# First stage of a fused conditional attention and MLP kernel: x blocks two and three requested behind the conditioning weights, the first transposes put into five banks, the second group's weights centred later

## The reference, cut to what matters

```
mod = swish(c) @ w_mod + b_mod            # six vectors of 576 for each of 2 batches
xn  = ln(x) * (1 + sc_msa) + sh_msa       # x: 2 x 2048 x 576
qkv = xn @ w_qkv + b_qkv                  # 16 heads of 36
q, k = ln(q, g_q), ln(k, g_k)             # over the 36 of a head
o   = softmax(q k^T / 6) v @ w_proj + b_proj
x   = x + g_msa * o
h   = gelu((ln(x) * (1 + sc_mlp) + sh_mlp) @ w1 + b1)
x   = x + g_mlp * (h @ w2 + b2)
```

## Time and profile before

| What | Value |
|---|---|
| Median of 3 runs (lowest, highest) | 2591.44 us (2589.94, 2591.81) |
| The profiled execution's own time | 2591.07 us |
| Its span on the core | 2589.3 us |
| PE busy | 2542.3 us, 98% of the span |
| DVE, ACT, POOL busy | 1871.6 us (72%), 1590.1 us (61%), 475.4 us (18%) |
| First score products of the attention on PE | at 97.33 us |
| First exponential on ACT | at 98.90 us |

### The profile page before, as it was taken

One profiled execution on the slowest core, in us unless ns is written; L12 is line 12 of the kernel. 1 busy time (PEld: TensorE's weight loads), 2 busy tenths in 40 slices (PEclk: granted clock), 3 DMA queues, 4 the chain that ended last, 5 costly groups with the idle time before them and its releaser, 6 DMA issues.

```text
span 2589.3 us, 41475 instructions
## 1 busy us (share of the span) xinstructions
PE 2542.3 (98%) x15223; PEld 1257.8 (49%) x15223; DVE 1871.6 (72%) x2950; ACT 1590.1 (61%) x2350; POOL 475.4 (18%) x334
## 2 busy tenths in 40 slices
PE   5999999999999999999999999999999999999999
PEld 3444444444444444444444433347566574756656
DVE  7788887788888788788777754275767667576743
ACT  4887787777777787888777776751423325142331
POOL 2532332223222222222322200001011010101100
PEclk9999999999999999999999999999999999999999
DMA  7513311223332133333111166356484856648443
GB/s 240 99 36 76 85 33 33 50 64 79 73 62 61 39 71 76 70 84 70 35 33 33 41 198 181 109 178 206 141 252 148 264 173 217 204 142 250 147 172 122
DMA packets 325888, 300.92 MB, mean 116 GB/s; under 512 B 235390, under 2 KB 267588, under 8 KB 313842
## 3 DMA queue, kind: packets, MB, share of 16 engines
q1 hardware_dynamic: 325394, 298.21, 41.4%
q10 hardware_dynamic: 288, 0.04, 0.0%
HBM read 203.84 MB, written 45.05 MB: 96 GB/s over the span
## 4 chain that ended last, share of the span: by engine, by line
PE 92%; DMA 2%; DVE 2%; SPq 1%; ACT 1%; issue 1%; POOL 0%; DVEq 0%; ACTq 0%
PE at_ps L1219 18%; PE at_ps L1202 17%; PE at_ps L2128 14%; PE at_ps L2085 14%; PE at_ps L1256 11%; PE at_ps L1230 8%; PE at_ps L1239 4%; PE at_ps L2056 4%; DMA ml_w_in<-in_L_cond_w 1%; PE at_ps L2078 1%; PE at_ps L2041 1%; DMA ml_held<-head_rden 0%; DMA st_wm_first<-in_L_cond_b_mod 0%; ACT at_aff L806 0%; PE at_ps L228 0%
## 5 line engine op out<-in xcount | busy, mean ns | idle before, releaser
L775 ACT ACTIVATE at_p<-at_ps 128x1024 f32<-128x1024 f32 x1024 | 1039.3, 1029 | 334.6 <-PE at_ps L1202 331.1
L1219 PE MATMUL at_ps<-at_p,at_v 128*37 128x512 f32 x2304 | 591.1, 593 | 0.0
L955 DVE TENSOR_TENSOR at_rest_of_p<-at_p,at_pr 128x1024 bf16<-128x1024 f32 x448 | 552.6, 1233 | 15.4
L642 POOL TENSOR_TENSOR at_tssq<-at_tssq,power 128x8 f32<-128x8 f32 x112 | 279.4, 2494 | 877.6 <-DVE at_tssq L918 877.0
L2085 PE MATMUL at_ps<-ml_xhi,ml_ring 128*128 128x512 f16 x1296 | 384.4, 381 | 2.9 <-ACT ml_g L1784 2.9
L2128 PE MATMUL at_ps<-ml_ring,ml_hid 128*128 128x288 f16 x3024 | 371.7, 286 | 0.8 <-issue 0.8
L947 DVE CAST at_pr<-at_p 128x1024 fp32r<-128x1024 f32 x448 | 315.2, 703 | 78.7 <-ACT at_p L775 77.6
L1230 PE MATMUL at_ps<-at_pr,at_vr 128*101 128x512 f32 x896 | 365.0, 488 | 1.3 <-DVE at_pr L947 1.2
L2128 PEld LDWEIGHTS at_ps<-ml_ring,ml_hid 128*128 128x128 f16 x3024 | 295.8, 98 | 75.9 <-issue 1.3
L1202 PE MATMUL at_ps<-at_qk_odd 109*64 109x512 f16 (+1 forms) x1658 | 309.4, 382 | 5.4 <-ACT at_p L775 5.4
L1202 PE MATMUL at_ps<-at_qk_even 109*64 109x512 f16 (+1 forms) x1536 | 308.7, 382 | 2.4 <-ACT at_p L775 2.4
(11 more groups left out here) (202 smaller groups left out, 2646.0 us busy)
## 6 DMA issues: line engine op xcount, KB each, us to landing
ml_ring<-w_halves SPq DMA_DIRECT2D x56, 1296.0 KB, 5.7
ml_ring<-w_halves SPq DMA_DIRECT2D x32, 1152.0 KB, 8.5
head_sums<-at_oT SPq DMA_DIRECT2D x256, 72.0 KB
ml_held<-head_sums SPq DMA_DIRECT2D x64, 256.0 KB
at_xy<-in_x SPq DMA_DIRECT2D x32, 288.0 KB, 2.9
ml_x<-in_x SPq DMA_DIRECT2D x8, 1152.0 KB, 10.2
w_halves<-ml_w_parts SPq DMA_DIRECT2D x18, 504.0 KB, 4.8
out<-ml_x SPq DMA_DIRECT2D x7, 1152.0 KB, 8.9
```

Of the source, the lines that this page charges most:

```text
L642: pool.tensor_tensor(tssq[:, 1, :], tssq[:, 1, :], keep.power[:, 0:QK], ALU.pow).then_inc(t_rstd, 1)
L775: act.activation(p[:, s % NP, :], ps[:, 2 * (s % 2):2 * (s % 2) + 2, :].rearrange("p a n -> p (a n)"), ACT.Exp).then_inc(exp_done, 1)
L955: nc.vector.tensor_tensor(rest_of_p[:, n % NL, :], p[:, s % NP, :], pr[:, n % NZ, :].bitcast(F32), ALU.subtract).then_inc(low_p_ready, 1)
L1219: last = nc.tensor.matmul(acc[a * HP:a * HP + RW, bank_of(U)], v32[:, (G % 2) * NT + 2 * s + a, h, :], p[:, s % NP, a * CH:(a + 1) * CH], ...
```

## The change

It edits five lists and one helper. SP: block 1 is requested when the first half of the conditioning weights has landed, block 2 behind it and ahead of group 1's weights, and block 3 ahead of `load_low`. PE: the transposes of block 0 write the banks 4, 5, 1, 2, 3 and wait for nothing; `product(0, 1)` stands ahead of block 1's first transposes; the last tile of block 0 is cut into two halves of 7 matmuls around the transpose of k = 4. DVE: block 1's statistics stand behind group 0's low parts, its normalising behind block 0's `low_x`, block 2's statistics earlier; `centre(1)` moves from behind block 0 to behind block 2, and `cut_low(1)` with its tail from the middle of block 2's `low_x` to behind `normal(0)`. ACT: `cut_high(1)` moves behind `square(1)`, and block 3's first cast waits for group 1's low parts, since it overwrites their place. POOL: block 1's `rstd_of` stands between the third and the fourth cast of block 0.

```
+        def turn_bank(t, k):
+            return 4 + (t * KC + k) % 2 if t else (4, 5, 1, 2, 3)[k]
@@ SP
             start.load_c(sp)
             load_x(0)
-            load_x(1)
             start.load_group(sp, 0)
             start.load_first(sp)
             sp.wait_ge(start.wm_loaded[0][0], 16)
+            load_x(1)
+            load_x(2)
             start.load_group(sp, 1)
-            load_x(2)
+            load_x(3)
             start.load_low(sp)
-            load_x(3)
             start.load_tail(sp)
@@ POOL
             rstd_of(0)
-            rstd_of(1)
             for k in range(KC):
                 pool.wait_ge(aff_ready, k + 1)
                 pool.tensor_copy(xhi[:, k, 0:CH], aff[:, k % 2, :]).then_inc(xhi_ready, 1)
+                if k == 2:
+                    rstd_of(1)
@@ ACT, affine
-                act.activation(aff[:, n % 2, :], ps[:, 4 + n % 2, :], ACT.Identity,
+                act.activation(aff[:, n % 2, :], ps[:, bank, :], ACT.Identity,
...
+                if t == NCH - 1 and k == 0:
+                    act.wait_ge(start.low, 2)
@@ ACT, the list
-            affine(1, 0)
-            affine(1, 1)
             raw(0)
-            affine(1, 2)
-            affine(1, 3)
-            affine(1, 4)
+            for k in range(KC):
+                affine(1, k)
             raw(1)
             square(0)
-            start.cut_high(act, 1)
-            start.cut_high_tail(act, 1)
...
             raw(3)
             square(1)
+            start.cut_high(act, 1)
+            start.cut_high_tail(act, 1)
             start.take_rows(act, 1)
@@ DVE
             stats_of(0)
-            stats_of(1)
             start.centre(dve, 0)
             normalise(0)
-            normalise(1)
             start.cut_low(dve, 0)
             start.cut_low_tail(dve, 0)
+            stats_of(1)
             for k in range(KC):
                 low_x(0, k)
-            start.centre(dve, 1)
-            start.gains(dve)
+            normalise(1)
+            stats_of(2)
             low_x(1, 0)
             low_x(1, 1)
-            stats_of(2)
             low_x(1, 2)
+            normalise(2, (0, 1))
             low_x(1, 3)
             low_x(1, 4)
-            normalise(2)
+            normalise(2, (2, 3))
+            start.gains(dve)
             sum_of(0)
@@ PE
-                    if n >= 2:
+                    if t:
                         pe.wait_ge(aff_ready, n - 1)
...
             first_product()
+            product(0, 1)
             turn(1, (0, 1))
-            product(0, 1)
+            product(0, 2)
             turn(1, (2, 3))
-            product(0, 2)
+            product(0, 3, range(0, 7))
             turn(1, (4,))
-            product(0, 3)
+            product(0, 3, range(7, 14))
```

More of the change, by code:

```diff
@@ L1139, in _ @@
             low_x(2, 4)
+            start.centre(dve, 1)
             normalise(3)
             normal(0)
+            start.cut_low(dve, 1)
+            start.cut_low_tail(dve, 1)
             sum_of(1)
```

15 lines of the change are left out of this document (7 added, 8 removed).

## The result

| | before | after |
|---|---|---|
| Median (12 executions each) | 2591.80 us | 2598.18 us |
| Lowest, highest | 2589.22, 2593.93 | 2595.67, 2599.98 |
| Profiled execution, its span | 2591.07, 2589.3 us | 2595.74, 2593.8 us |
| First scores on PE | 97.33 us | 99.94 us |
| First exponential on ACT | 98.90 us | 103.44 us |

A forecast was written before the change was run, and what follows sets the result against it. It took PE to hold 92% of the chain, with the stage going from wait to wait; +4.4 at conditioning, -0.8 POOL, -2.2 block 3's DVE list gave 1.4 us gained, so 2590.0 us, 8-in-10 range 2587.0 to 2592.9.

The forecast's parts named there:

- Conditioning: Start of the stage: PE finishes the conditioning products at 25.15 instead of 29.52, 4.4 us earlier.
- the bound of 26.3: Block 1's x on DVE: landing after 26.3 us decides for the case of a slower kernel.
- The slower rival: Block 1's x lands late, delaying DVE's statistics and the first `xlo`; 2592.0, or 2593 with 10 us; 17%.
- POOL's root: Block 1's add and power between POOL's third and fourth casts make block 0's fifth piece 0.8 us late.
- 0.45 to the end of the first tile: PE in block 0: after the last `low_x`, 0.45 us to finish the first token tile.
- PE falls to the slow pace: Rival: PE's clock drops in the thin stretch between 25 and 35 us, 0.7 us off the gain, 2590.7; 5%.
- Five banks: PE's transposes of block 0 into five banks: costed at nothing, `xlo` pieces still every 1.20 us.
- Block 3's list: DVE's work behind `centre(1)`, 12.35 us, ends at 75.1, so `affine(3, 2)` comes 1.4 us earlier than before.
- POOL's powers come at their old distance from DVE's sums: End of the stage: POOL's powers keep their old delay behind DVE's sums, with no cost added.
- Behind `affine(3, 2)` the change leaves every list as it was: From `affine(3, 2)` to the scores nothing changes, so only that start is asked for; 1.4 us gained.
- Nothing arrives: Rival: waits in DVE's late list or POOL's power of `sum_of(1)` cost 1.4 more; 2591.4; 20%.
- The main account: Late centring in block 3's DVE list takes back the rest of the front's lead, leaving 1.4 us.

The follow-up runs named there:

- e3: Changed kernel with 14 extra matmuls filling the waits of PE's first product in block 0; median 2598.26 us, ratio 1.0024 to the kernel before.
- e11: Changed kernel with block 1's root behind the casts, `sum_of(1)` ahead of `cut_low(1)`, `vr` cleared later, and the filling matmuls of e3 and e6; ratio 1.0007.
- e12: e11 with `centre(1)` on DVE ahead of block 2's low parts instead of behind them; ratio 1.0002 to the kernel before.
- e10: Kernel before the change, with POOL clearing `vr` five times instead of once, between power(1) and power(2); ratio 1.0013.
- e2: Changed kernel with DVE doing `sum_of(1)` ahead of `cut_low(1)` and its tail instead of behind them; ratio 1.0014 to the kernel before.
- e4: Kernel before with only the late centring: `centre(1)`, `cut_high(1)`, `cut_low(1)` moved, block 3's first cast waiting; median 2599.39 us, ratio 1.0026.
- e6: Changed kernel with 16 extra matmuls on PE between the first and third score products; ratio 1.0016 to the kernel before.

## Why the prediction was wrong

It forecast 2590.0 with 2587.0 to 2592.9, no change to be told. Each row of the table is a stretch in which a term of it went wrong. The lead over the kernel before, in us:

| Place | Predicted | Measured | Lost on the way |
|---|---|---|---|
| First `xlo` | 4.4 | 3.35 | 1.05 |
| Block 1's last `xlo` | 3.8 | 0.84 | 1.9 |
| Block 2's last `xlo` | 6.0 | 2.64 | 0.4 |
| `affine(3, 2)` | 1.4 | -2.61 | 0.65 |
| First exponential | 1.4 | -4.54 | 1.9 |

- **Conditioning** (25.15, "4.4 us earlier"). The first half was right to 0.03. For the second, the wait of 1.34 was taken out of the distance between the halves, for no reason but that this is the earliest case. The halves start 5.09 us apart, 5.39 before, and PE waits 1.58 us between them. Mis-sized, by 1.05.
- **Block 1's x** landed 0.5 us before the bound of 26.3. DVE waited 0.69 us for it, to 25.83, and this reached nothing, by 0.1 us: DVE's statistics end at 29.34, and the first `xlo` is 6.39 us behind conditioning's second half in both kernels (23.06 to 29.45, 26.41 to 32.80). The slower rival was not what happened.
- **POOL's root** ("I take 0.8"). Right: the fifth piece ends at 35.67 with 2.61 of lead, 0.74 less than the first. What failed is the next step, "0.45 to the end of the first tile". PE needs 2.25, since its last eight matmuls come in one heap and at the lower clock (1.46 us at the other pace, 2.79 measured). The rival "PE falls to the slow pace" (5%) was what happened, at this place; e3 prices the pace at 1.3, where the prediction had 0.7 behind a slack of 1.3. There is no slack: PE runs from 35.13 to 47.9 without a gap, so all of it goes to block 1's last `xlo`, at 49.36 for 46.4 (its terms add up to 46.3). The prediction had seen that PE is thinly used there "as before". It isn't quite as before. In the kernel before PE still transposes block 0's last three pieces while the `xlo` begin, and starts the first product only at 34.91, when two pieces wait for it already. Two rows, of the kernel before:

```profile
32.15 1.32 PE L1269 MATMUL at_ps<-ident,at_y 128*128 128x128 f32 x8 [1.15 <-ACT at_aff L806]
...
34.91 0.35 PE L1288 MATMUL at_ps<-at_wq,at_xhi 128*128 128x432 f16 x1
```

The change does these transposes ahead, from 27.57. That this thinning brings the dip is likely and not proven: all nine traces with the new front and no filling matmuls have it, the three with them (e3, e11, e12) don't, but the old front has it in e10.

- **Five banks**: as costed for the cycle of `affine`, cast and `low_x`; each of the first three pieces still comes at 1.20 us. Their side effect on PE, just named, was not in the sum.
- **Block 3's list** ("12.35 us" behind `centre(1)`). The items were right but for `normalise(3)`, 3.66 us for 2.9, with POOL's clearing of `stk` now beside it. From the measured end of block 2 the prediction's 16.2 us give 78.5, and it was 79.14.
- **The last step is the one that failed as reasoning**: the path behind `affine(3, 2)`, whose change was put at nothing. "POOL's powers come at their old distance from DVE's sums", "Behind `affine(3, 2)` the change leaves every list as it was. So I ask only how much earlier `affine(3, 2)` starts." The prediction named `sum_of(1)` moving behind `cut_low(1)`, and even a rival for its power "about 1.5 us later", but followed only what ACT waits for. POOL's chain of power(1), clearing, power(2) stands beside `affine(3, 2)`, starts with `sum_of(1)`, and had 3.0 us of slack in it (2.45 + 0.58, e10). The sum came 5.07 us late; 1.2 of this lies in the prediction's own list (it puts `sum_of(1)` at 71.0, 69.72 before), the rest is the lead lost further ahead and the 0.65. Since the stage itself is 2.61 late at `affine(3, 2)`, the lateness alone would make a wait of only some 0.2 us beyond the slack; POOL's add and power, slower beside `normal(1)`, make the rest of the 2.14. e2 takes the wait away and e10 makes one anew. The rival "Nothing arrives" (20%) named both places of this loss, DVE's list and POOL's power, but priced them at 1.4 together, where the exponential came 4.54 later than before.

The 2% for slower was too small for a sum in which a lead of six microseconds is handed back by a list that ends level to 0.1: several terms stood at their early end, and nothing in the stage could pay for one that came late. The main account, that the late centring gives back in block 3 what the front gains, was right in its place; it gives back 5.25 (e4: 5.4), where 4.6 were in the sum, and three further terms of one to two microseconds (conditioning, the first tile, POOL's powers) turned the rest into a loss.

## What to carry to other kernels

Work that is moved off one wait is still owed: add it up where it lands, and follow every engine's chain from there to the end, not only the one that waits last now; a chain off the path has a slack that can be read (2.45 + 0.58 us here), and in e10 6.0 us more work in it came out as a wait of 2.89. Allow for its instructions getting longer where they fall beside another engine's. Independent work that stands in PE's short waits held its clock up here (e3, e6), so moving transposes out of a thin stretch can cost more than their own time. And where several terms are taken at their favourable end, the forecast is a bound and not a middle.
